# A second softmax mixer and a root product, laid between the turns of a relation edge stage (one Trainium2 core)

## The reference

```python
xn = _layernorm(x, axis=-1)
x = x + _L1_gnn_ref(xn, edge_index, edge_type_8, edge_weight, ...) + _L1_mix_ref(xn[None], ...)[0]
...
# _L1_gnn_ref: 8 relations
msg = x[src] * edge_weight[:, None]
seg = edge_type * N + dst
sums = jax.ops.segment_sum(msg, seg, num_segments=R * N)
h = sums / jnp.maximum(cnt, 1.0)[:, None]
out = jnp.einsum('rnc,rco->no', h.reshape(R, N, C), weight)
out = out + x @ root + bias
...
# _L1_mix_ref: 4 heads of 32 channels, 4 memory slots
qkv = rmsnorm(x, g_pre) @ w_qkv
q = jax.nn.softmax(q, axis=-2) * SCALE          # over the 32 channels of a head
k = jax.nn.softmax(concat(mk, k), axis=-1)      # over all nodes and the 4 slots
context = jnp.einsum('bhdn,bhen->bhde', k, v)
out = jnp.einsum('bhde,bhdn->bhen', context, q)
return rmsnorm(out @ w_out + b_out, g_out) + x
```

## Time and profile before

| | us |
|---|---|
| median of 3 runs (7699.64 to 7709.82) | 7706.6 |
| profiled execution | 7706.61 |
| its span, first to last instruction | 7704.9 |
| relation tables, last table store issued | 3201.74 |
| root stage, first load issued | 3214.26 |
| edge stage, first record load issued | 3247.21 |
| edge stage, last addition to the accumulator starts | 3918.69 |
| addition of the accumulator to X | 3919.79 to 3928.26 |
| mixer | 3929.26 to 4089.49 |
| second feed-forward, first operation | 4090.38 |

### The profile page before, as it was taken

How to read it: one execution, slowest core, us unless ns; L and a number is a source line. 1 busy time by engine, 2 the same in 40 slices (tenths; PEclk the granted TensorE clock), 3 DMA queues, 4 the chain that set the end, 5 groups by cost and what they waited for, 6 DMA issues and landing times. The chain is left out here.

```text
span 7704.9 us, 74434 instructions
## 1 busy us (share of the span) xinstructions
PE 4594.6 (60%) x18357; PEld 3419.3 (44%) x18357; DVE 3425.1 (44%) x7895; ACT 1891.0 (25%) x4727; POOL 3734.1 (48%) x3581
## 2 busy tenths in 40 slices
PE   0160666666664974778854915554469748875628
PEld 0030444444443761366643813332358636664515
DVE  6830777777776125433344143323621152224461
ACT  0000555555552210033311200001022114431201
POOL 0776777777771651077712637770034347770000
PEclk9985777777776987887766957776689967777659
DMA  0011444444441662233432323361046423362000
GB/s 36 14 52 28 123 121 123 121 123 125 120 124 40 205 168 72 114 103 103 100 30 61 92 65 105 105 97 23 3 153 191 148 70 103 104 92 25 1 20 17
DMA packets 391531, 677.74 MB, mean 88 GB/s; under 512 B 127759, under 2 KB 258093, under 8 KB 387656
## 3 DMA queue, kind: packets, MB, share of 16 engines
q0 software_dynamic: 188992, 431.92, 23.6%
q1 hardware_dynamic: 202170, 241.74, 9.7%
HBM read 591.29 MB, written 81.90 MB: 87 GB/s over the span
## 5 line engine op out<-in xcount | busy, mean ns | idle before, releaser
L905 POOL DMA_INDIRECT g0e_got<-g_table,g0e_rc x496 | 594.3, 1198 | 293.3 <-issue 156.8
L690 POOL DMA_INDIRECT g1e_got<-g_table,g1e_rc x496 | 489.4, 987 | 477.2 <-DMA g1e_rc<-rec_dst 326.4
L907 POOL DMA_INDIRECT g0e_keyed<-g_keys,g0e_rc x496 | 569.0, 1147 | 166.7 <-issue 166.7
L690 POOL DMA_INDIRECT g3e_got<-g_table,g3e_rc x496 | 491.7, 991 | 255.9 <-issue 146.5
L690 POOL DMA_INDIRECT g2e_got<-g_table,g2e_rc x496 | 474.1, 956 | 261.1 <-issue 147.4
L753 PE MATMUL g2e_pa<-g2e_got,g2e_placew 128*125 128x256 f32 x992 | 364.3, 533 | 321.9 <-issue 210.2
L257 POOL DMA_INDIRECT rec_dst<-bydst_rc,bydst_sloti x391 | 393.3, 1006 | 294.4 <-DVEq L449 175.6
L943 ACT ACTIVATE g0e_spaced<-g0e_spread 125x512 bf16<-125x512 f32 x992 | 499.1, 625 | 21.8 <-PE g0e_spread L979 18.6
L1849 PE MATMUL f_p<-f_w2s,f_hid 128*128 128x256 f32 (+1 forms) x2176 | 493.1, 383 | 12.6 <-ACT f_hid L1869 1.7
L1838 PE MATMUL f_p<-f_xt,f_w1s 128*128 128x256 f32 (+1 forms) x2176 | 491.1, 383 | 15.4 <-DMA f_b2s<-in_L_ffn_b 10.3
L969 PE MATMUL g0e_pt<-g0e_new,g0e_placet 125*128 125x8 f32 x992 | 207.3, 337 | 489.0 <-DVEq L1039 489.0
(11 more groups left out here) (597 smaller groups left out, 8756.6 us busy)
## 6 DMA issues: line engine op xcount, KB each, us to landing
f_w1s<-in_L_ffn_W SPq DMA_DIRECT2D x32, 1024.0 KB
f_w2s<-in_L_ffn_W SPq DMA_DIRECT2D x32, 1024.0 KB
g_table<-g1t_out SPq DMA_DIRECT2D x25, 1000.0 KB
f_w1s<-in_L_ffn_w SPq DMA_DIRECT2D x40, 512.0 KB
f_w2s<-in_L_ffn_w SPq DMA_DIRECT2D x40, 512.0 KB
f_results<-f_y SPq DMA_DIRECT2D x72, 256.0 KB
f_b2s<-in_L_ffn_b SPq DMA_DIRECT2D x80, 128.0 KB
f_rows<-XN SPq DMA_DIRECT2D x3, 3125.0 KB
```

Source lines behind the costliest of these rows:

```text
L690: pool.indirect_dma_start(got[:, g % GOTS, j, :], None, table, bass.IndirectOffsetOnAxis(rc[:, g * GT + j, idx:idx + 1], 0))\
L905: pool.indirect_dma_start(got[:, s, j, :], None, table, bass.IndirectOffsetOnAxis(rc[:, sl, j, R_IDX:R_IDX + 1], 0)).then_inc(got_in[s], 16)
L907: pool.indirect_dma_start(keyed[:, s, j, :], None, keys, bass.IndirectOffsetOnAxis(rc[:, sl, j, R_KEY:R_KEY + 1], 0)).then_inc(got_in[s], 16)
```

## The change

The root stage, `add_stage` and the mixer's own stages are gone. `edge_stage` takes a `side`, an object whose `scalar`, `tensor` and `vector` methods are Python generators: at the end of each turn an engine's program advances its generator by one step, and what the step contains stands behind the turn's own instructions. `SoftmaxMixer` holds the mixer and the root product, cut by node tile. The sums of the edge stage are added to X in place of a cleared accumulator. XN, which the mixer adds to X, goes in with the root product: the identity is added to the root matrix (`root + I`). The transposed queries overwrite chunk 0 of `R.XNT`, tile by tile, behind their last use.

Per engine, with a step a turn: VectorE scales the weights and sets constants in turn 1; projects tile t in turn 4 + 2t (with the end of the softmax of the queries of tile t-1), adds the root product in turn 5 + 2t, up to turn 53; the maximum of the keys over all nodes in turns 54 to 57; subtracts it from two key tiles a turn, turns 57 to 69; context and output matrix in turns 71 to 73; one output tile a turn in turns 74 to 99. TensorE's steps stand one turn ahead of VectorE's that take them, but in turns 56 and 57, where both are in the same turn. ScalarE has twelve squares a turn in turns -1 and 0, then an exponential or a copy a turn, and a square and a root a turn at the end. Turns 100 to 123 have no step.

In PSUM the side work takes four banks; the edge stage keeps one bank for transposes, one for the spread product and two for sums.

```diff
-def edge_stage(nc, R, name, mode, b, acc, width, table, idx=R_IDX, spread=None):
+def edge_stage(nc, R, name, mode, b, acc, width, table, idx=R_IDX, spread=None, side=None, clear=True):
...
+    turns, adds = (2, 4) if side is None else (1, 2)
...
                 sp.dma_start(rc[:, at, :], view[:, at, :]).then_inc(rec_in[c], 16)
+            if side is not None:
+                side.sync(sp)
...
         @block.tensor
+            own = side.tensor(pe) if side is not None else None
             for n in range(-3, groups):
...
-                    if g >= 2:
-                        pe.wait_ge(evacuated, g - 1)
+                    if g >= turns:
+                        pe.wait_ge(evacuated, g - turns + 1)
...
-                    if g >= 2:
-                        pe.wait_ge(logit, g - 1)
+                    if g >= turns:
+                        pe.wait_ge(logit, g - turns + 1)
...
-                        if j % each == 0 and x >= 4:
-                            pe.wait_ge(added, x - 3)
+                        if j % each == 0 and x >= adds:
+                            pe.wait_ge(added, x - adds + 1)
...
+                advance(own)
+            run_out(own)
...
         @block.vector
-            dve.memset(acc, 0.0)
+            if clear:
+                dve.memset(acc, 0.0)
...
     with ExitStack() as ctx:
-        w = ctx.enter_context(nc.sbuf_tensor("g1_root", [128, KC, D], F32))
...
-        rows_stage(nc, R, "g1root", w[:, :, :], D, finish_root,
-                   loads=[(w[:, :, :], chunks_of(a["L1_gnn_root"], D)), (b[:, :], row_of(a["L1_gnn_bias"], P))])
-    with ExitStack() as ctx:
-        acc = ctx.enter_context(nc.sbuf_tensor("g1_acc", [P, NT * D], F32))
-        edge_stage(nc, R, "g1e", "relation", by_dst, acc[:, :], D, table, idx=R_ROW, spread=R.inv_count[:, :])
-        add_stage(nc, [(R.X, acc)])
+        edge_stage(nc, R, "g1e", "relation", by_dst, R.X[:, :], D, table, idx=R_ROW, spread=R.inv_count[:, :],
+                   side=SoftmaxMixer(nc, R, ctx, a), clear=False)
...
-        with nc.cleanup_on_exit():
-            softmax_mixer(nc, R, "m1", a["L1_mix_w_qkv"], a["L1_mix_w_out"], a["L1_mix_b_out"], a["L1_mix_g_pre"],
-                          a["L1_mix_mem_kv"], a["L1_mix_g_out"])
```

More of the change, by code:

```diff
@@ L695, in _ @@
         def _(act):
-            if not spreads:
-                return
+            own = side.scalar(act) if side is not None else None
             for n in range(-3, groups):
                 g = n + 1
-                if 0 <= g < groups:
+                if spreads and 0 <= g < groups:
                     act.wait_ge(logit, g + 1)
@@ L712, in _ @@
                 g = n + 3
-                if g < groups:
+                if spreads and g < groups:
                     act.wait_ge(turned, g + 1)
@@ L726, in _ @@
                     pe.wait_ge(placed, g + 1)
-                    if g >= 2:
-                        pe.wait_ge(evacuated, g - 1)
+                    if g >= turns:
+                        pe.wait_ge(evacuated, g - turns + 1)
                     for j in range(GT):
-                        last = pe.transpose(pt[g % 2][:, j * 128:(j + 1) * 128], place[:, g % 4, j, :], identb[:, :])
+                        last = pe.transpose(pt[g % turns][:, j * 128:(j + 1) * 128], place[:, g % 4, j, :], identb[:, :])
                     last.then_inc(turned, 1)
@@ L741, in _ @@
                             at = pe.snap(tile_reg)
-                        last = pe.matmul(pq[g % 2][:, j, 0:sw], placet[:, g % 4, j, :], spread[:, ds(at * sw, sw)],
+                        last = pe.matmul(pq[g % turns][:, j, 0:sw], placet[:, g % 4, j, :], spread[:, ds(at * sw, sw)],
                                          start=True, stop=True)
@@ L760, in _ @@
             tile_reg = dve.alloc_register(f"{name}_dve_tile")
-            dve.memset(acc, 0.0)
+            own = side.vector(dve) if side is not None else None
+            if clear:
+                dve.memset(acc, 0.0)
             dve.tensor_copy(identb[:, :], R.identf[:, :])
@@ L795, in _ @@
                         dve.drain()
-                        dve.tensor_tensor(small[:, g % 2, :, :], pq[g % 2][:, 0:GT, :], rel[:, g % 2, :, :], ALU.mult)
+                        dve.tensor_tensor(small[:, g % 2, :, :], pq[g % turns][:, 0:GT, :], rel[:, g % 2, :, :], ALU.mult)
                         dve.drain()
@@ L818, in _ @@
                         into = acc[:, ds(to * width, width)]
-                        dve.tensor_tensor(into, into, pa[x % 4][:, 0:width], ALU.add)
+                        dve.tensor_tensor(into, into, pa[x % adds][:, 0:width], ALU.add)
                         dve.drain().then_inc(added, 1)
+                advance(own)
+            run_out(own)
 def attention_edge_stage(nc, R, name, table, keys, masks_in, acc):
```

282 lines of the change are left out of this document (268 added, 14 removed).

## The result

| | us, median (range) | ratio to before |
|---|---|---|
| before | 7708.2 (7699.6 to 7713.9) | 1 |
| after | 7528.8 (7526.5 to 7532.2) | 0.9769 [0.9752, 0.9785] |

The changed kernel is 179.4 us faster, 2.3%. The forecast was 7508 us, 21 us lower. The time lies above the 7497 to 7520 us that the forecast gave itself with a chance of 0.60, and in the part of the range, up to 7560, that it left to rival (a), beside that rival's second form, 7525 us. The profiled execution of after took 7526.5 us; its span is 7524.8 us, 180.1 less than that of before (7704.9).

What follows compares the result with a forecast made beforehand. GpSimd's issue of gathers, 5.15 us a group, was taken to set the edge stage's pace, with some 20 us of slack for TensorE. 7706.6 - 203.3 - 2.7 + 4 + 3 = 7507.6, say 7508 us; range 7497 to 7520.

Steps and rivals of the forecast that it cites:

- rival (a): Edge stage: turns spill over; first form has the clock mixed, 6.3 us a projection turn, 7550 us; chance 0.32.
- second form: Edge stage: VectorE's operations 0.3 us dearer a turn, clock high, 75 turns, 22 us more lag, about 7525 us.
- Removed, 203.3 us: Root stage (32.95 us), plus accumulator sum into X and whole mixer (170.4 us), leave the path.
- The first gather, -2.7 us: Edge stage start: without the accumulator's memset GpSimd's first gather no longer takes 3.62 us; saves 2.7 us.
- Gathers slowed by VectorE, +4 (0 to 14): Edge stage: VectorE's added operations with both inputs in SBUF slow GpSimd's gathers; +4 us, range 0 to 14.
- The start, 12 to 13 of the slack used: Edge stage start: first sum, loads and squares leave TensorE lagging by 12 to 13 of 20 us slack.
- VectorE's projection turn, 5.24 us: Edge stage, 50 projection turns: VectorE's own and added work averages 5.24 us a turn against GpSimd's 5.15.
- 0 to 15 us of lag: Edge stage: TensorE's clock mostly high, with spells at the low level worth 0 to 15 us of lag.
- +3 us of waiting: End of the projections: lag of 15 to 30 against 20 us slack makes GpSimd wait 0 to 10; +3 taken.
- Turns 56 and 57, "less 4": Light turns give back 15 to 20 us, less 4 where VectorE waits twice for a product of the same turn.
- (b): Edge stage: TensorE's clock stays low all through, +179 us, about 7685 us; chance 0.04.
- (c): Edge stage: serial handshakes, side steps in full between turns, 10.1 us a projection turn, 7820 us; chance 0.03.

Runs made afterwards that it cites:

- tile_early: Changed kernel with VectorE's load of the tile number issued between the place operation and the wait for its end, instead of behind it; 7511.6 us, ratio 0.9736.
- hands_apart: Changed kernel with TensorE's two products around the key maximum one turn earlier (turns 55 and 56); 7527.2 us, ratio 0.9757.

## Why the prediction came out as it did

**Removed, 203.3 us:** right. The root stage, the mixer and the addition of the accumulator are gone: the records are asked for 12.5 us behind the last table store, and the next layer begins 1.24 us behind the last addition. Counted from border to border, the profiled execution changed by -203.33 + 16.74 + 3.97 + 0.35 + 2.17 = -180.10 us; this sum closes by construction and says where the time lies, not why.

**The first gather, -2.7 us:** right. It takes 1.29 us, not 3.62, and ends 5.2 us behind the load of the records where it ended 7.7 behind before; the forecast "near 0.95" missed that a place operation runs beside it now.

**Gathers slowed by VectorE, +4 (0 to 14):** too much; it came to nothing. Without the one blocked gather before (2.7 us, which the forecast's 21 us of excess had counted in) it was 486.7 us for 496, now 486.2. The longest still takes 1457 ns beside a place, so the effect is there. But the place met fewer starts, 64 of 496 in place of 84, which cost 14.8 us in place of 17.5, and the new operations, being short, cost 1.4. That the two offset each other was not foreseen. The Trainium skill's rule in "SBUF — State Buffer", "Who interferes with whom", would have given 0 for this term, which is what it came to, though for a reason that the 1457 ns contradict; the whole sum would then be 7503.6 us, farther from the measured time.

**The start, 12 to 13 of the slack used:** about right. The squares take 0.58 us each with the reading of their sum (forecast 0.45), TensorE waited 4.9 us for ScalarE once, and the sum of group 4 started 15.1 us behind the end of its gathers, where in the kernel before it is 2.0 in the steady state (3671.90 to 3673.86): 13 us. The slack was a little more than put: the first two waits of GpSimd were for sums that started 23.8 and 25.7 us behind their gathers, 22 to 24 above those 2.0. The forecast took 20, though its own figures, 26 less 3.9, give 22.

**The step that failed: VectorE's projection turn, 5.24 us.** It was 5.54, and 50 x 0.30 = **15 us** of lag. Of the 0.30, 0.12 is under-counted work (4.35 + 6.36 against 4.31 + 6.16 for two turns): above all the three scalings, which take 0.86 us (3328.50 to the end of the third at 3329.36) where 0.71 was put, and 0.19 us ahead of the first. The other 0.18, 9 us in all, are turns at the low clock: 7.4 us of it is the time that VectorE stood before its additions beyond 0.99 us each (56.9 less 49.5), and the gaps like that at 3331.62, two in 50 turns, come to 0.7. tile_early shows it more plainly. It took 5.23 us over an undisturbed 5.02 (3381.33 to 3385.32 and on to the next place at 3391.36), 10.6 us in 50 turns, and its additions stood 39.6 us where 50 x 0.58 = 29.0 is usual, 10.6 more:

```profile
L1147 DVE TENSOR_TENSOR X<-X,g1e_pa 125x256 f32 x50 | 21.0, 421 | 39.6 <-PE g1e_pa L1073 23.0 <-issue 16.6
```

The forecast had the spells at the low clock as "0 to 15 us of lag", and then took +3 us of waiting from an interval of 0 to 10: it took the low end of a term whose middle was 7 to 8. With 9 us for them and 6 for the work, its own account of lag gives 13 + 4.5 + 15 = 32 against 20 to 24, so 8 to 12 us of waiting.

**Turns 56 and 57, "less 4":** right in the mechanism, mis-sized, and put where it costs nothing. The forecast took the 4 us from what the light turns give back. They cost 7.3, and they come before the light turns, when the slack is used up. hands_apart gave 10.0 us for them. These and the projection turns are the 21.2 us of waiting, in place of 3. The last 25 turns with a step took 5.56 us (138.9 in all) where 5.4 was forecast; that cost nothing, since by then the light turns had given the slack back.

**Rivals:** (a) came true in its second form: its "0.3 us dearer a turn and the clock high" are the measured 0.30 and 0.92, its 7525 us the 7528.8. That is partly luck: only 0.12 of the 0.30 are dearer operations, and it had them in 75 turns, not 50. Its first form, the clock mixed at 6.3 us a turn, did not; nor did (b) or (c): serial handshakes occurred in two turns of 124. The chance of 0.32 for (a) was too low beside 0.60 for a forecast that had no room for its own 0 to 15. The low end, too, is not what its words give: 7500.6 less 5 is 7496, and 7497 stands there, which decides nothing.

**The signs named in advance:** clock over 0.85 in the projections, 0.92, but 0.74 to 0.83 from the last phase on; VectorE 62 of 100 us, right; GpSimd's waits under 15 us, wrong, 28.4; VectorE's turn over 5.4 with no idle time, which was named as the sign of being wrong, came half true: the turn is over 5.4, but VectorE did wait for TensorE in ten turns, and without that it would be 5.4. The first gather (1.29 in place of 0.95) and the hand-over (1.24 in place of 0.9) missed by 0.3 us each.

## What to carry to other kernels

Where one engine sets the pace and another serves it through a ring of buffers, keep two numbers: how many microseconds the server may fall behind, and how many it does, turn by turn; as long as the second is below the first, added work is free, and from there on each microsecond counts in full. A turn 2% over the pace (5.24 against 5.15) leaves nothing for irregular turns over 50 turns, and these, which no list of instructions shows, add 3% here (5.36 to 5.54). When the slack is gone, several repairs bring back in part the same microseconds: here three took 10.8, 9.1 and 14.9 us off the waiting, 35 in all, of 21 that were to be had. All of them together were not run on a chip without the stops. So the cheapest may do: look for idle time in the bound engine's own turn, such as a register load behind an operation that it could run beside.

## What the runs showed of the hardware

A register load issued while VectorE still worked on the place operation took 0.41 us off the gap of 0.99 us between place and addition (0.58 left), not the 0.68 that the operation lasts.

An indirect gather that starts while VectorE's comparison of 128x500 runs, with both inputs in on-chip memory, takes longer by about what is left of that operation less 0.12 us: in the kernel before 84 of 496 gathers started so, which cost 17.5 us in all, up to 0.5 us each. One that started during the memset of 125x6400 took 3.62 us and ended 0.92 us behind it.

A stretch in which TensorE's granted clock is mostly high can still be lengthened by the rest: at 0.92 over 277 us, ten sums of 2.7 to 3.8 us in place of 1.97 held up VectorE for 7 us.

And runs on different chips differ: on two of the four used here the same kernel takes 8144 to 8176 us in place of 7714 to 7716, in the traces there with stops of mostly 2 to 3.5 us, often 20 us apart, that no wait of the program explains. The edited kernels gain 1.7 to 1.8% there; the changed kernel as it is was not run on them.
